# Splitting the second layer's kernels and first rows in the last quad, and moving three convolutions

## The reference

```python
# layer 0: an embedding picks a mixture of 8 expert matrices per batch, then a 2048x2048 product with a low-rank update
out = jnp.einsum('boi,bih->boh', agg_w, x) + agg_b[:, :, None]
out = jnp.einsum('bsd,od->bso', x, W) + bias          # plus A, Bf with coeffs * scales
# layer 1: grouped convolution (4 groups, 9 taps), bias per batch and channel, then a gathered feed-forward
out = lax.conv_general_dilated(x, weight, (1,), [(4, 4)], feature_group_count=4)
t = t[:, perm].reshape(b * l, 16, 128)
t = jnp.einsum('bhd,hdm->bhm', t, up); t = gelu(t); t = jnp.einsum('bhm,hmd->bhd', t, down)
t = t.reshape(b * l, 2048)[:, unperm]
# x = x + layer0(x); x = x + layer1(x)
```

## Time and profile before

| | us |
|---|---|
| median of 3 runs (2629.69 to 2630.16) | 2629.75 |
| the profiled execution | 2630.83 |
| its span | 2629.0 |
| TensorE busy in the span | 2568.3 (98%) |
| VectorE busy | 1829.9 (70%) |
| ScalarE busy | 1001.6 (38%) |
| granted TensorE clock, mean | 0.993 |

### The profile page before, as it was taken

One profiled execution on the slowest core, in us unless ns is written; L12 is line 12 of the kernel. 1 busy time (PEld: TensorE's weight loads), 2 busy tenths in 40 slices (PEclk: granted clock), 3 DMA queues, 4 the chain that ended last, 5 costly groups with the idle time before them and its releaser, 6 DMA issues. The chain is left out here.

```text
span 2629.0 us, 39103 instructions
## 1 busy us (share of the span) xinstructions
PE 2568.3 (98%) x12090; PEld 2108.8 (80%) x12090; DVE 1829.9 (70%) x2667; ACT 1001.6 (38%) x1631; POOL 954.8 (36%) x826
## 2 busy tenths in 40 slices
PE   8899999999999999999999999999999999999997
PEld 6678888888888888887888778888888888888775
DVE  6555555865555854566444668888888888888876
ACT  3211211312122322233222455555555555555573
POOL 2265644456553454332232312222222222222321
PEclk9999999999999999999999999999999999999998
DMA  9955544756544777576555664476767677777787
GB/s 308 315 179 181 198 163 155 264 176 204 180 159 170 238 227 216 173 239 203 161 163 180 199 180 132 144 223 205 223 208 224 211 219 221 222 219 217 214 275 241
DMA packets 417283, 541.02 MB, mean 206 GB/s; under 512 B 36249, under 2 KB 270065, under 8 KB 417073
## 3 DMA queue, kind: packets, MB, share of 16 engines
q1 hardware_dynamic: 315584, 307.40, 39.3%
q10 hardware_dynamic: 77376, 154.27, 15.6%
q0 software_dynamic: 24112, 76.80, 9.2%
HBM read 309.72 MB, written 228.61 MB: 205 GB/s over the span
## 5 line engine op out<-in xcount | busy, mean ns | idle before, releaser
L434 PE MATMUL ps_c<-w_hi,ring_hi 128*128 128x512 f32 x1792 | 713.7, 398 | 6.8 <-DVE w_lo L848 3.9
L434 PE MATMUL ps_c<-w_hi,ring_lo 128*128 128x512 f32 x1792 | 707.4, 395 | 0.0
L434 PE MATMUL ps_c<-w_lo,ring_hi 128*128 128x512 f32 x1792 | 707.3, 395 | 0.0
L585 ACT ACTIVATE ring_hi<-raw_n 128x512 fp32r<-128x512 f32 x384 | 240.7, 631 | 896.5 <-DVE raw_n L883 247.6
L1297 POOL DMA_INDIRECT y_d<-y_s,idx x128 | 146.8, 1147 | 726.1 <-ACT y_s L1465 679.1
L434 PEld LDWEIGHTS ps_c<-w_hi,ring_hi 128*128 128x128 f32 x1792 | 338.3, 189 | 85.7 <-issue 6.6
L1432 ACT ACTIVATE kern<-ps_up 128x512 f32<-128x512 f32 x512 | 306.6, 599 | 259.0 <-PE ps_up L1315 245.8
L434 PEld LDWEIGHTS ps_c<-w_hi,ring_lo 128*128 128x128 f32 x1792 | 337.8, 189 | 79.0
L434 PEld LDWEIGHTS ps_c<-w_lo,ring_hi 128*128 128x128 f32 x1792 | 338.3, 189 | 75.9
L1549 DVE TENSOR_TENSOR g_lo<-kern,g_hi 128x512 fp32r<-128x512 f32 x512 | 354.7, 693 | 38.5 <-ACT g_hi L1436 22.0
L939 DVE TENSOR_TENSOR r_early<-ps_c,r_early 128x512 f32<-128x512 f32 x256 | 176.8, 691 | 285.3 <-PE ps_c L434 285.3
(11 more groups left out here) (197 smaller groups left out, 3838.0 us busy)
## 6 DMA issues: line engine op xcount, KB each, us to landing
u_d<-raw_n ACTq DMA_DIRECT2D x64, 512.0 KB, 3.2
x_d<-r_early ACTq DMA_DIRECT2D x128, 256.0 KB, 3.4
x_d<-x_s ACTq DMA_DIRECT2D x128, 256.0 KB, 2.7
raw_n<-u_d SPq DMA_DIRECT2D x64, 512.0 KB, 3.7
u_s<-x_d SPq DMA_DIRECT2D x496, 64.0 KB, 3.2
z_d<-x_s SPq DMA_DIRECT2D x120, 256.0 KB
rear<-y_d SPq DMA_DIRECT2D x112, 256.0 KB, 3.1
rear<-x_d SPq DMA_DIRECT2D x112, 256.0 KB
```

The source lines that it names most:

```text
L434: mm = nc.tensor.matmul(bank, a[:, dc, :], w[k][:, dc, :], start=(first and dc == 0 and n == 0), stop=(dc == 3 and n == 2), skip_group_che ...
L585: nc.scalar.activation(ring_hi[g % RING][:].rearrange("p a n -> p (a n)"), ring_raw[p][k], ACT.Copy).then_inc(hi_ready, 1)
```

## The change

The kernels and the rows of units 0 and 1 are split in the last quad of layer 0, in slots 10 to 13. The tiles for them stand where layer 0's tiles are free by then. Layer 0's TensorE list gets the convolutions of units 0 and 1 behind its last product; layer 1's list leaves them out. Unit 20's convolution and the turn of unit 19 move from step (0, 0) to the end of the step before it, ahead of the two waits and the first up product. `load_weights` waits for a semaphore of the kernels' own. In the lead the convolutions now write two banks of `ps_up` in turn, and the second set of row buffers is a pair of its own (`xt_hi`, `xt_lo`), which later serves as `t_hi`, `t_lo`.

```diff
+        def layer1_split(q, t):
+            if q != QUADS - 1:
+                return (), ()
+            return {10: ((0,), (0,)), 11: ((1,), (1,)), 12: ((2,), ()), 13: ((3,), ())}.get(t, ((), ()))
...
             quads(slot)
+            for u in range(2):
+                pe.wait_ge(sh.cwlo_ready, u + 1)
+                pe.wait_ge(sh.xlo_ready, u + 1)
+                hi, lo = first_xp[u]
+                for tau in range(3):
+                    for n, (w, rows) in enumerate(((cw_hi, hi), (cw_hi, lo), (cw_lo, hi))):
+                        mm = nc.tensor.matmul(sh.ps_up[:, u, :], w[:, 3 * u + tau, :], rows[:, tau:tau + Q],
+                                              start=(tau == 0 and n == 0), stop=(tau == 2 and n == 2))
+                mm.then_inc(sh.conv_done, 1)
...
+            def split_kernel(g):
+                if g == 0:
+                    act.wait_ge(sh.cw_in, 16 * 12)
+                    act.wait_ge(lo_ready, LAST - 2)
+                    act.wait_ge(u_mm, 4 * QUADS // 2)
+                    act.wait_ge(u_ready, 4 * QUADS // 2)
+                nc.scalar.activation(cw_hi_flat[:, kernel_part[g]], kern[:, kernel_part[g]], ACT.Copy).then_inc(sh.cwhi_ready, 1)
+            def split_rows(u):
+                act.wait_ge(sh.xp_in[u], 64)
...
+                nc.scalar.activation(first_xp[u][0], sh.xp[u], ACT.Copy).then_inc(sh.xhi_ready, 1)
...
                 for n in freed_chunks(q, t):
                     split_early(n)
+                kernels, rows = layer1_split(q, t)
+                for g in kernels:
+                    split_kernel(g)
+                for u in rows:
+                    split_rows(u)
...
             def load_weights(n):
-                pool.wait_ge(wsplit_lo, G + max(n - 3, EARLY))
+                pool.wait_ge(wsplit_lo, max(n - 3, EARLY))
+                pool.wait_ge(sh.cwlo_ready, G)
...
             def conv(k, h):
                 u, j, b, g = conv_unit(k, h)
-                if isinstance(k, int) and 0 <= u < G:
-                    pe.wait_ge(wsplit_lo, EARLY + g + 1)
+                if isinstance(k, int) and u < 2:
+                    return
+                if isinstance(k, int) and u < G:
+                    pe.wait_ge(sh.cwlo_ready, g + 1)
...
             def step(k, h, parity):
-                if exists(k, h, LEAD):
-                    conv(k, h)
-                if exists(k, h, LEAD - 1):
-                    turn_z(*before(k, h))
+                if not isinstance(k, int) or H * k + h != 0:
+                    if exists(k, h, LEAD):
+                        conv(k, h)
+                    if exists(k, h, LEAD - 1):
+                        turn_z(*before(k, h))
...
                 if isinstance(k, int) and H * k + h == -1:
-                    pe.wait_ge(wsplit_lo, G + CHUNKS)
+                    conv(0, 0)
+                    turn_z(k, h)
+                    pe.wait_ge(wsplit_lo, CHUNKS)
                     pe.wait_ge(z_ready, LEAD)
...
-            act.wait_ge(sh.cw_in, 16 * 12)
-            split_kernel(0)
-            act.wait_ge(sh.pad_ready, 3)
-            split_x(-2, 2 * H - LEAD)
-            for g in range(1, G):
-                split_kernel(g)
```

More of the change, by code:

```diff
@@ L43 @@
 RING = 6
+XP_GAP = 156
 LAST = QUADS * ITEMS
@@ L174, in layer0_block @@
         r_early = sb("r_early", [P, 4, 512])
+        next_xp = ExitStack()
+        sb("below_xp", [P, XP_GAP], F32, next_xp)
+        sh.first_xp = [[sb(f"{x}_{n}", [P, Q + 2], F32R, next_xp) for n in ("hi", "lo")] for x in ("xp", "xt")]
+        next_xp.close()
+        first_xp = [[t[:] for t in pair] for pair in sh.first_xp]
         s1 = sb("s1", [P, 2, 512])
         mix = sb("mix", [P, 4, 256])
+        with ExitStack() as next_up:
+            sh.ps_up = next_up.enter_context(nc.psum_tensor("ps_up", [P, MC, 512], F32))
         ps_v = ctx.enter_context(nc.psum_tensor("ps_v", [P, 2, HALF], F32))
@@ L200, in layer0_block @@
         w_stage = [x_n2[:, j // 2, j % 2 * 512:(j % 2 + 1) * 512] for j in range(4)]
+        kernel_part = [slice(3 * g * P, 3 * (g + 1) * P) for g in range(G)]
+        cw_hi_flat, cw_lo_flat = cw_hi[:].rearrange("p a b -> p (a b)"), cw_lo[:].rearrange("p a b -> p (a b)")
         CW = G * 3 * P
@@ L1000, in layer1_block @@
         o_s = [results[:, j, :] for j in range(2)]
+        (xp_hi, xp_lo), (xt_hi, xt_lo) = sh.first_xp
+        for n in range(4):
+            sb(f"xp_room{n}", [P, Q + 2])
+        t_hi, t_lo = xt_hi[:, 0:RB], xt_lo[:, 0:RB]
         idx = sb("idx", [P, H], I32)
@@ L1007, in layer1_block @@
                    rear[:].rearrange("p w (s c) -> p w s c", s=S)]
-        ps_up = bank("ps_up", MC)
+        ps_up = sh.ps_up
+        bank("up_room", MC)
         ps_c, ps_zt, ps_y, ps_f = bank("ps_c"), bank("ps_zt"), bank("ps_y"), bank("ps_f")
@@ L1089, in chunks_of, with conv_bank @@
             return range(n, n + 2) if EARLY <= n < CHUNKS else ()
+        def conv_bank(k, h):
+            return ps_up[:, h % 2, :] if lead(k) else ps_c[:, 0, :]
         def pair_of(k, h):
@@ L1101, in t_pair @@
                 return xp_hi[:, 0:RB], xp_lo[:, 0:RB]
-            return t_hi[:], t_lo[:]
+            return t_hi, t_lo
         def xp_of(k, h):
@@ L1394, in _ @@
         def _(act):
[L1395 to L1399, removed]
             def split_weights(n):
```

47 lines of the change are left out of this document (27 added, 20 removed).

## The result

The changed kernel takes **2644.19 us** (median of 5 runs, 2640.38 to 2648.15) against 2629.75 before. The ratio is 1.0058, 95% interval 1.0047 to 1.0069: slower by 0.58%, where 2631.4 was forecast and "slower" had a chance of 0.05. The profiled execution ran 2646.61 with a span of 2644.7, so 15.7 us more span than before.

The account below looks back on a forecast made before the run. TensorE, busy 98% of the span, was taken as the bound, so only its idle or low-clock places could give anything. The seam's +2.4 and unit 20's −0.7 made +1.7 us on 2629.75: 2631.4 us, range 2628.4 to 2634.9.

Parts of the forecast that it names:

- The bank and tile moves: New places for tiles and convolution banks: forecast to cost nothing, as the same instructions run in the same number.
- The seam: Between layer 0's last product and layer 1's convolutions: +2.4 us, from a low clock behind a 6.9 us wait for unit 2.
- the landing of unit 2's rows: Behind the barrier at the seam: row transfers taken to land in 2.4 us, so unit 2 starts at 1505.8, no later.
- rival 3: At the seam, unit 2's rows queue behind the weight loads: +4.2 us, so 2635.6; chance 0.04.
- The low clock: Behind the wait for unit 2: 4.3 to 5.7 us at low clock, 49% lost, taken as 2.4 us.
- Splits in the last quad: Kernel and row splits in slots 10 to 13 of layer 0's last quad: no cost, 0.6 us at the far end.
- Unit 20: Its convolution ahead of the first up product: −0.7 us from three up matmuls at full clock, if the clock stays up.
- the wait that I had forecast for step (0, 0): Sign to look for: in step (0, 0), 2 to 3 us of waiting for DVE ahead of the next up product.
- rival 1: The clock is also low at unit 20's convolution: +1.6 us instead of −0.7, so 2633.7; chance 0.27.
- Rival 2: At the seam, the barrier doesn't wait for TensorE's matmuls: −1.3 us, so 2628.4; chance 0.11.

Follow-up runs that it names:

- e1: The changed kernel with padding alone, putting its tiles at the offsets modulo 128 bytes of the kernel before; 2635.90 us, ratio 1.0028.
- e4: The changed kernel with GpSimd's four weight loads at the head of layer 1 waiting until unit 2's rows are split; 2642.81 us, ratio 1.0051.
- e8: e1 with unit 2's rows loaded in quad 25 instead of in layer 1's block behind the barrier; 2632.85 us, ratio 1.0017.
- e7: e1 with unit 20's convolution and unit 19's turn back in step (0, 0), behind the first up product; 2632.62 us, ratio 1.0015.
- e5: The kernel before with 64 bytes of padding ahead of layer 0's ring; 2617.41 us, ratio 0.9957.
- e6: e5 with the convolution's rows xp_hi and xp_lo also moved to offset 96; 2611.81 us, ratio 0.9939.
- e9: The edits of e1, e7 and e8 together, with the ring moved as in e5; 2614.24 us, ratio 0.9949.
- e3: The kernel before with 64 bytes of padding ahead of all weights and 64 more ahead of xp_hi; 2639.58 us, ratio 1.0036.
- e2: The kernel before with 192 bytes of padding ahead of g_hi, moving all tiles behind it too; 2636.63 us, ratio 1.0028.
- e10: The kernel before with t_lo alone moved by 32 bytes; 2635.46 us, ratio 1.0025.

## Why the prediction was wrong

**The step that failed** is the sentence "The bank and tile moves cost nothing: the same instructions in the same number." The count was right and the conclusion was not. The moves made each of the steps 20 to 56 0.093 us longer, which is 10.3 us from step 0 to step 108, and e1 took it back by padding alone. No rival held it, since I had looked for costs only where TensorE waits. The page could have raised the question: the mean duration of one and the same kind of matmul differs by the tiles that it reads, 390 ns for `t_lo` by `w_hi` (above) against 394 for this group, with nothing waiting:

```profile
L1315 PE MATMUL ps_up<-t_hi,w_lo 128*128 128x512 f32 x472 | 185.8, 394 | 0.0
```

 The Trainium skill's page "TensorE: Matmul & The Clock Gate" (section "Wait — 56ns, not 53.3ns?") gives back-to-back matmuls of 512 columns one figure at the full clock, 215.7 ns. No row here shows that: nine took 2.13 us, 0.237 each, and it is this pace that went with the places. The Trainium skill's page "SBUF — State Buffer" (section "Operand start alignment") asks of an operand's start only that it be a multiple of the element's size, and says that this is about legality, not speed. All the places above satisfy it, and the runs show that they differ in time.

**The seam: +2.4 forecast, +4.07 measured.** The 18 matmuls at the full clock, the barrier held up by them, a low clock in units 2 and 3: all came. The barrier opened 0.28 us behind TensorE's end, not 0.68. The mis-sized term is the landing of unit 2's rows, 4.6 instead of 2.4, so that unit 2 came 1.87 later than before, not 0. I had named the weight loads as what could do it (rival 3), and weighed it with a transfer that took 2.7 beside them, keeping the 4.9 of the earlier trace rows only as the far end, 1508.26; e4 showed 2.1 without them, and in e8 unit 15's result went to memory 4.5 us earlier than in e1 (53.62 and 58.16 behind the last product). The fixed cost of 2.0 us that the prediction takes from the Trainium skill's page "DMA: Bandwidth & Descriptors" stands in a section on GpSimd's queue; the rows here are SyncE's, and without the loads they landed in 2.0 to 2.1. The low clock cost 2 × 0.43 × 7.2 × 49% = 3.0 instead of 2.4. Together 4.9. A later gap was 0.5 shorter (0.77 us at 1528 instead of 1.26), but that gap varies from 0.74 to 1.42 among the kernels with the old seam, so this is a matter of the execution. The remaining 0.3 I did not trace.

**Splits in the last quad: nothing, right.** TensorE kept its pace to the last product and VectorE's last sum did not hold the barrier.

**Unit 20: −0.7 forecast, +1.7 measured.** The convolution ran at the full clock after 1.40 us of idle (forecast 1.7), and the next up product gained what three matmuls at the full clock give (4.85 − 4.17 = 0.68). Two things were missing. The gather took 4.19 us instead of 3.39, which made the first up product 0.8 later still. That goes with the move: the gather took 3.33 to 3.44 us in the eight kernels whose unit 20 is convolved behind the first up product, and 3.73 to 4.40 in the four where it is ahead (after, e1, e4, e8). Why it is slower with TensorE at work beside it is not shown. And the wait that I had forecast for step (0, 0), "2 to 3 us for DVE", came with 2.83 us, but I had not asked of it what I had asked of the others, whether it lowers the clock. It did: the clock of the stretch behind it was 0.79, and step 0's copy lost another 1.58. That is rival 1's mechanism, one wait later than it was put. Together 0.8 − 0.68 + 1.58 = 1.7. e7 against e1 gives the same 1.7: 0.97 in the gather (3.36 and 4.33), 0.73 from the first up product to step 0's copy (13.08 and 13.81).

**Rival 2** (the barrier does not wait) is refuted by SyncE's first issue at 1498.53. Without the failed step the forecast would still have been 5 us off: e1, the change at the old places, is 6.7 slower than before, where +1.7 was forecast, and at 2635.90 it lies above the range (to 2634.9). So the landing and the low clock in step (0, 0) were failures of their own, smaller ones.

## What to carry to other kernels

A tile that moves in SBUF is an edit of every matmul that reads it. Compare the mean durations of the busiest groups, or the distance of one instruction from itself some steps on, and if they moved without a wait, put padding in until the operands stand as they did. Try the offsets of the busiest loop on purpose, and measure: 64 bytes of padding ahead of the ring were worth more here (10 to 16 us) than the whole reordering, and the rule that led to them held only in part.

Work that is moved out of a wait leaves a wait behind it. Where the chain that ends it starts at a barrier or a gather, ask what the moved work covered, and what the clock does behind each gap that is new.

## What the runs showed of the hardware

- Steps 20 to 56 took 305.04 us in seven of the kernels (before, e1, e5, e6, e7, e8, e9), 308.40 in three (after, e3, e4), 307.68 and 307.20 in e2 and e10. The start of layer 0's last product varies by 6 us between kernels whose ring was not moved (1490.1 to 1496.4), these steps do not vary at all, so 0.01 us a step can be read from one profile. Further on it is less exact: steps 56 to 108 took 441.87 to 442.37 in the same seven.
- The pace of back-to-back 128x512 matmuls depends on where tiles start in SBUF: the `_lo` halves of the up and down products took 389 to 391 ns with 64 bytes between their operands modulo 128 (before, e1) and 397 in the changed kernel. It depends on more than a matmul's own operands: `t_lo` by `w_hi` went from 390 to 397 when only `g` and the tiles behind it moved (e2).
- The same matmuls with the same tiles at the same places ran at two paces in one execution of e5: 439 of them in 100 us, later 431, both at the full clock.
- Four row transfers of 64 KB landed in 2.0 to 2.1 us without four loads of 256 KB beside them (before, e4) and in 3.5 to 4.6 us with them (after).
- The barrier between the blocks opened 0.28 us behind the end of the last matmul.
- The gather ahead of the first up product took 3.33 to 3.44 us in the eight kernels with unit 20 behind it (TensorE was busy for 0.34 us of it in the kernel before), and 3.73 to 4.40 in the four with unit 20's convolution beside it (2.79 us in the changed kernel).
- A gap of 1.40 us and one of 1.19 us left the clock at 2.4 GHz (granted 1.00 in both stretches); after two more, of 1.12 and 2.83 us, the stretch behind them had 0.79.
